# The experts' gathers without a bound: empty slots read the last row of the node table

## The chip, the cores and the metric

The kernel runs on one core of a Trainium2 chip. The metric is the device time of the whole program in microseconds. The core's engines are TensorE (PE; its weight loads are PEld), VectorE (DVE), ScalarE (ACT), GpSimd (POOL) and SyncE (SP); 16 DMA engines move data between HBM and the on-chip memories.

## The reference

A graph convolution over 6250 nodes with 256 features and 200000 edges, a mixture of 64 experts of which each node takes two, then two normalisations. Cut to what matters:

```python
h = feats * rsqrt(deg_out)[:, None]
m = segment_sum(h[src], dst) * rsqrt(deg_in)[:, None]
x = (m @ W_gc + b_gc) + (feats @ W_res + b_res)      # 6250 x 256: the node table
vals, idx = top_k(x @ Wg + bg, 2); gates = softmax(vals)
# every node's row goes to its two experts, at most 1024 rows each (CAP)
h1 = gelu(einsum('ecd,edh->ech', buf, w1) + b1)      # 64 experts, 256 -> 512
h2 = einsum('ech,ehd->ecd', h1, w2) + b2             # 512 -> 256
y = x + sum_k gate_k * h2[row of the node's k-th choice]
out = layernorm(feats + batchnorm(y) * gamma + beta)
```

A row of an expert's buffer that no node takes has no effect on the output.

## The kernel before

The program has four stages, one after the other.

**Degrees and table.** Histograms of `src` on TensorE give the out-degrees; the scaled node features go to HBM as `table`, of NPAD = 49 x 128 = 6272 rows of 256 floats (1 KB).

**Edges** (to about 2200 us). The 200000 edges lie in columns of 128. There are 1568 columns, 196 groups of CPG = 8; 200000 / 128 = 1562.5 columns hold edges, and the rest was filled with PAD_SRC = NPAD - 1 = 6271 (`dve.memset(raw_src[:, EB - 1, :], PAD_SRC)`, L706). GpSimd issues one indirect DMA per column (`gather`, L465), which fetches 128 rows of `table`, with no bound. TensorE adds them up by destination with one-hot matmuls (L1154). Whenever a tile of 128 nodes is complete, "ticks" on all engines compute its `x`, its experts and the ranks of its rows within them, and ScalarE stores `x` to HBM as `nodes` (L608), all 128 rows of each of the 49 tiles, so that row 6271 of `nodes` is written too.

**Slot tables.** One-hot matmuls (L1173) build in two PSUM banks, for each of 64 x 8 chunks of 128 slots, which node and which choice stand in each slot. VectorE makes two index tables of it (L963 to L976): `sidx`, the row of the result table `y2` that the slot's output goes to, and `gidx`, the row of `nodes` that it reads. An empty slot gets UNUSED = 1e6 in `sidx`, and a number far above the last row in `gidx`. `slots_ready` then lets GpSimd go on, and `tables_done` the others.

**Experts** (about 2229 to 2810 us). The choices are 2 x 6250 = 12500 in 64 experts, 195 on average. Each expert has MAIN = 3 chunks whose DMAs are always issued, and a loop for the chunks above the third (`extra_chunks`). For each expert:

- SyncE loads w1, w2 and b2 of the expert after next, double buffered by parity (`weights`, L375, L380, L381).
- GpSimd, in its own order: the extra chunks of expert e, the three gathers of expert e + 2 (`load_slots`, L489; behind `tokens_t`, which says that the buffer `xg` of that parity has been transposed), and the three scatters of expert e (`store_slots`, L499; each behind its `out_ready`). Both kinds carry a bound, with `oob_is_err=False`: an index above the bound moves nothing. The bound of the gathers is N - 1 = 6249, that of the scatters the last row of `y2`.
- TensorE (`expert`, from L1272): layer 1 of the chunks that hold rows (L1263), then the transposes of expert e + 1 (`transpose_tokens`, L1256; chunk by chunk behind `gathered[par][k]`, and of all three chunks, empty or not), then layer 2 (L1269).
- ScalarE applies gelu (L663), VectorE copies the transposed tokens to SBUF (L1003, L1004) and adds b2 (L1030).

Since a skipped slot leaves the buffer as it was, GpSimd clears `xg` and `xgx` once before the first gather, with two memsets (L477, L478). Both lie in `ring_low`, the buffers of the edge phase.

**Combination and normalisation** (from about 2820 us): the rows of `y2` are read back, weighted and added, and the two normalisations follow.

What sets the order around the change is each engine's own instruction stream; semaphores tie the streams together, and nothing is reordered.

Of the kernel before, what the change touches and what calls it, by code (L numbers as in the profile page):

```python
# [9 lines left out]
ALU = mybir.AluOpType  # L10
# [5 lines left out]
N, D, EDGES = 6250, 256, 200000  # L16
H, EX, TOPK, CAP = 512, 64, 2, 1024
# [3 lines left out]
NPAD = NT * P  # L21
# [18 lines left out]
PAD_SRC = NPAD - 1  # L40
# [17 lines left out]
def graph_moe_kernel(nc, x, src, dst, W_gc, b_gc, W_res, b_res, Wg, bg, w1, b1, w2, b2, gamma, beta, out):  # L58
    ctx = ExitStack()
    with ctx:  # L60
        def sb(name, shape, dt=F32):
            return ctx.enter_context(nc.sbuf_tensor(name, shape, dt))

        def sem(name):
            return ctx.enter_context(nc.semaphore(name))
# [85 lines left out]
        tok_f = hot_low[:, :, :].rearrange("p j d -> p (j d)")[:, 0:SC]  # L151
        tok_t = hot_low[:, :, :].rearrange("p j d -> p (j d)")[:, SC:2 * SC]
        gidx, sidx = slots[:, 0, :], slots[:, 1, :]
# [15 lines left out]
        def piece(n):  # L169
            taken_to[0] += n  # L170
            return arena[:, taken_to[0] - n:taken_to[0]]

        xg = piece(2 * MAIN * D).rearrange("p (b k d) -> p b k d", b=2, k=MAIN)
# [3 lines left out]
        xgx = piece(D)  # L177
# [8 lines left out]
        xtra_idx = sb("xtra_idx", [P, 2], I32)  # L186
# [43 lines left out]
        nd_pick, nd_rank, nd_sel, nd_slot = sem("nd_pick"), sem("nd_rank"), sem("nd_sel"), sem("nd_slot")  # L230
        y2_zeroed = sem("y2_zeroed")
        nd_stored = sem("nd_stored")
        slots_mm, tokens_clear, slots_ready = sem("slots_mm"), sem("tokens_clear"), sem("slots_ready")
        tables_done, gb_in, gap_ready, exp_ready = sem("tables_done"), sem("gb_in"), sem("gap_ready"), sem("exp_ready")
        b1_t = sem("b1_t")
        w1_in, w2_in, b2_in = ([sem(f"{w}_in{par}") for par in range(2)] for w in ("w1", "w2", "b2"))
        gathered = [[sem(f"gathered{par}{k}") for k in range(MAIN)] for par in range(2)]
# [6 lines left out]
        xtra_copied, xtra_gathered, xtra_t, xtra_s = sem("xtra_copied"), sem("xtra_gathered"), sem("xtra_t"), sem("xtra_s")  # L244
# [173 lines left out]
        def _(pool):  # L418
# [19 lines left out]
            pool.memset(acc_flat[:, 0:2 * COLS], 0.0).then_inc(acc_zero, 1)  # L438


            node_reg, row_reg = pool.alloc_register("last_node"), pool.alloc_register("last_row")
            pool.reg_mov(node_reg, N - 1)
            pool.reg_mov(row_reg, TOPK * NPAD - 1)
            last_node, last_row = node_reg, row_reg

            def start():
                pool.sem_inc(pool_starts, 1)
# [26 lines left out]
            pool.wait_ge(y2_zeroed, 16 * (TOPK * NPAD // P // 2))  # L474
            pool.wait_ge(nd_stored, 16 * NT + 16)
            pool.wait_ge(slots_mm, 1)
            pool.memset(xg[:, :, :, :], 0.0).then_inc(tokens_clear, 1)  # L477
            pool.memset(xgx[:, :], 0.0).then_inc(tokens_clear, 1)  # L478
            pool.wait_ge(tokens_clear, 2)
            pool.wait_ge(slots_ready, 1)  # L480

            def load_slots(e, par, first):

                if not first:
                    pool.wait_ge(tokens_t, e - 1)
                    start()
                for k in range(MAIN):
                    col = e * SLOTCH + k
                    pool.indirect_dma_start(  # L489
                        out=xg[:, par, k, :], out_offset=None, in_=nodes[:, :],  # L490
                        in_offset=bass.IndirectOffsetOnAxis(ap=gidx[:, col:col + 1], axis=0),
                        bounds_check=last_node, oob_is_err=False).then_inc(gathered[par][k], 16)

            def store_slots(e, par):
                for k in range(MAIN):
# [11 lines left out]
            def extra_chunks(e, nch):  # L507
                with pool.If(nch > MAIN):
                    with pool.Fori(MAIN, nch) as k:
                        col = nc.s_assert_within(k + e * SLOTCH, 0, SC - 1,  # L510
                                                 skip_runtime_bounds_check_because="no expert has more than SLOTCH chunks")
                        pool.reg_add(nextra, nextra, 1)
                        n = pool.snap(nextra, min_val=1, max_val=EX * SLOTCH)
                        pool.tensor_copy(xtra_idx[:, 0:1], gidx[:, bass.ds(col, 1)])
                        pool.tensor_copy(xtra_idx[:, 1:2], sidx[:, bass.ds(col, 1)]).then_inc(xtra_copied, 1)
                        pool.wait_ge(xtra_copied, n)
                        start()
                        pool.indirect_dma_start(
                            out=xgx[:, :], out_offset=None, in_=nodes[:, :],
                            in_offset=bass.IndirectOffsetOnAxis(ap=xtra_idx[:, 0:1], axis=0),  # L520
                            bounds_check=last_node, oob_is_err=False).then_inc(xtra_gathered, 16)
                        pool.wait_ge(xtra_out, n)
                        start()
                        pool.indirect_dma_start(
                            out=y2[:, :], out_offset=bass.IndirectOffsetOnAxis(ap=xtra_idx[:, 1:2], axis=0),
                            in_=outx[:, :], in_offset=None,
                            bounds_check=last_row, oob_is_err=False).then_inc(xtra_scattered, 16)
                        pool.wait_ge(xtra_scattered, n * 16)
                        start()

            def chunks_of(e):
                return pool.value_load(nch_i[0:1, e:e + 1], min_val=1, max_val=SLOTCH)

            load_slots(0, 0, True)
            load_slots(1, 1, True)
            pool.wait_ge(tables_done, 1)
            for e in range(EX):
                extra_chunks(e, chunks_of(e))
                if e + 2 < EX:
                    load_slots(e + 2, e % 2, False)  # L540
                store_slots(e, e % 2)
# [163 lines left out]
        def _(dve):  # L705
# [97 lines left out]
            a, k = 0, 1  # L803
            while k < GROUPS:
                dve.drain()
                dve.tensor_tensor(sfx[:, 1 - a, 0:GROUPS], sfx[:, a, 0:GROUPS], sfx[:, a, k:GROUPS + k], ALU.min)
                a, k = 1 - a, 2 * k
# [165 lines left out]
            dve.drain()  # L973
            dve.tensor_tensor(tok_f, tok_f, tok_t, ALU.add)
            dve.drain()
            dve.tensor_copy(gidx[:, :], tok_f).then_inc(slots_ready, 1)  # L976

            dve.tensor_scalar(nch_f[:, :], banks[5][0:1, 2 * P:2 * P + EX], float(CAP), float(P - 1), ALU.min, ALU.add)
            dve.drain()
# [391 lines left out]
```

## Time and profile before

| | us |
|---|---|
| median of 3 runs | 3005.2 |
| lowest and highest | 3001.09, 3006.76 |
| the profiled execution | 3007.82 |
| its span, first to last instruction | 3006.0 |

| engine | busy us | share of the span |
|---|---|---|
| TensorE matmuls | 2070.9 | 69% |
| GpSimd | 1948.3 | 65% |
| VectorE | 1251.7 | 42% |
| ScalarE | 395.3 | 13% |

The shares are means over stages with different limits: the edge phase is a steady stream of gathers on GpSimd, the experts' stage is denser on TensorE. A view by window tells one stage from another; the waits say who waited for whom; the chain of waits is the one path of work and waits that led to the end, so a delay counts there and not elsewhere.

### The profile page before, as it was taken

To read this page: it belongs to the slowest core of one execution; us is meant where nothing else is said; L and a number is where in the kernel's file an instruction comes from. 1 tells how busy PE (TensorE), PEld (TensorE's weight loads), DVE (VectorE), ACT (ScalarE), POOL (GpSimd) and SP (SyncE) were. 2 spreads that over 40 slices of the span, in tenths; PEclk is the share of its full clock that TensorE was granted. 3 is DMA by queue.
4 is the path that set the end of the run, shared out by engine and by line. 5 is a ranking of instruction groups with operands and counts; after the bars stand their busy time and mean duration, and the time that the engine had idled before them with its cause. 6 is when DMAs were issued, how large, how long until landed. Compare 5 with 4: busy or idle time off the path is not lost.

```text
span 3006.0 us, 44273 instructions
## 1 busy us (share of the span) xinstructions
PE 2070.9 (69%) x10262; PEld 1708.5 (57%) x10263; DVE 1251.7 (42%) x3095; ACT 395.3 (13%) x1350; POOL 1948.3 (65%) x1989
## 2 busy tenths in 40 slices
PE   7955656566666666666766777777768898989360
PEld 6954444444544455555555555655647787989250
DVE  9971112223233333444445444555542222222467
ACT  1010000000000000010111111111112222323013
POOL 2007777777777777777777777777725577777603
PEclk6557777777778788888889998999978899999685
DMA  8023333333333333333333333333424465656332
GB/s 291 0 95 106 107 106 106 106 107 107 107 108 109 108 109 108 109 109 111 109 109 111 111 111 111 111 111 111 111 72 138 147 192 179 199 182 196 107 121 85
DMA packets 205321, 363.40 MB, mean 121 GB/s; under 512 B 43160, under 2 KB 125894, under 8 KB 205054
## 3 DMA queue, kind: packets, MB, share of 16 engines
q0 software_dynamic: 93888, 231.34, 26.8%
q1 hardware_dynamic: 104058, 123.31, 12.8%
q10 hardware_dynamic: 7108, 6.43, 0.6%
q14 instruction: 250, 2.05, 0.2%
q8 instruction: 17, 0.28, 0.0%
HBM read 328.57 MB, written 57.52 MB: 128 GB/s over the span
## 4 chain that ended last, share of the span: by engine, by line
POOL 35%; PE 27%; issue 18%; DVE 8%; DMA 5%; DVEq 3%; ACT 1%; POOLq 1%; PEld 1%; ACTq 1%; SPq 0%; PEldq 0%
POOL ring L465 17%; POOL stage L465 17%; PE bank L1269 7%; PE bank L1154 6%; PE bank L1263 6%; PE bank L1134 3%; DMA ring<-nodes,slots 2%; PE bank L1194 2%; DVE acc L1047 1%; PE bank L1256 1%; DMA stage<-y 1%; PE bank L1173 1%; DVE stage L756 1%; DMA ring<-table,ring_idx 1%; DVE slots L856 1%
## 5 line engine op out<-in xcount | busy, mean ns | idle before, releaser
L465 POOL DMA_INDIRECT ring<-table,ring_idx x792 | 749.0, 946 | 241.8 <-issue 240.6
L465 POOL DMA_INDIRECT stage<-table,ring_idx x776 | 733.9, 946 | 236.3 <-issue 233.4
L1154 PE MATMUL bank<-ring,hot 128*128 128x257 f32 x1056 | 305.8, 452 | 166.8 <-DMA ring<-table,ring_idx 157.9
L1154 PE MATMUL bank<-stage 128*128 128x257 f32 x1040 | 305.9, 458 | 137.6 <-DMA stage<-table,ring_idx 128.9
L1154 PEld LDWEIGHTS bank<-ring,hot 128*128 128x128 f32 x1056 | 237.7, 231 | 229.0 <-issue 151.1
L1154 PEld LDWEIGHTS bank<-stage 128*128 128x128 f32 x1040 | 237.8, 234 | 200.0 <-issue 106.2
L952 DVE TENSOR_TENSOR acc<-acc,bank 128x257 f32 x196 | 82.9, 423 | 564.4 <-PE bank L1154 526.9
L499 POOL DMA_INDIRECT y<-ring,slots x192 | 193.3, 1007 | 98.3 <-issue 58.8
L1263 PEld LDWEIGHTS bank<-ring,stage 128*128 128x128 f32 x1984 | 236.9, 196 | 16.4 <-issue 11.8
L1263 PE MATMUL bank<-ring,stage 128*128 128x128 f32 x1984 | 241.0, 281 | 6.4 <-issue 3.7
L489 POOL DMA_INDIRECT ring<-nodes,slots x192 | 195.6, 1019 | 68.5 <-issue 55.6
L1269 PE MATMUL bank<-stage,ring 128*128 128x256 f32 x976 | 229.5, 389 | 7.5 <-ACT ring L663 7.5
L1154 PE MATMUL bank<-ring,stage 128*128 128x257 f32 x528 | 160.2, 469 | 105.1 <-DMA ring<-table,ring_idx 67.8
L1154 PE MATMUL bank<-stage,hot 128*128 128x257 f32 x512 | 157.5, 474 | 90.1 <-DMA stage<-table,ring_idx 84.4
L1269 PEld LDWEIGHTS bank<-stage,ring 128*128 128x128 f32 x976 | 185.7, 196 | 34.1 <-issue 10.2
L1154 PEld LDWEIGHTS bank<-ring,stage 128*128 128x128 f32 x528 | 124.0, 241 | 138.8 <-issue 58.4
L1154 PEld LDWEIGHTS bank<-stage,hot 128*128 128x128 f32 x512 | 121.7, 244 | 123.5 <-issue 79.3
L663 ACT ACTIVATE ring<-bank,b1e 128x128 f32<-128x128 f32 x488 | 139.1, 368 | 379.8 <-PE bank L1263 379.8
L589 ACT ACTIVATE ring_idx<-srcT 128x8 int32 (+1 forms) x198 | 40.1, 205 | 962.9 <-DMA ring<-table,ring_idx 487.9
L1134 PE MATMUL bank<-stage 128*128 128x49 bf16 x1568 | 159.9, 278 | 7.3 <-DVE stage L756 6.8
L1134 PEld LDWEIGHTS bank<-stage 128*128 128x128 bf16 x1568 | 153.0, 150 | 14.2 <-DVE stage L756 13.3
L1003 DVE COPY ring<-bank 128x512 f32<-128x512 f32 x64 | 44.2, 691 | 260.1 <-PE bank L1256 251.0
(230 smaller groups left out, 2551.0 us busy)
## 6 DMA issues: line engine op xcount, KB each, us to landing
stage<-in_L_gnn_w_dram SPq DMA_DIRECT2D x128, 512.0 KB
ring<-table,ring_idx POOLq DMA_INDIRECT x792
y<-zeros SPq DMA_DIRECT2D x49, 256.0 KB, 2.1
stage<-y SPq DMA_DIRECT2D x14, 896.0 KB, 7.3
stage<-table,ring_idx POOLq DMA_INDIRECT x776
stage<-in_L_gnn_b_dram SPq DMA_DIRECT2D x64, 128.0 KB
nodes<-yS ACTq DMA_DIRECT2D x49, 128.0 KB
xs<-in_x_dram SPq DMA_DIRECT2D x1, 6144.0 KB
```

Of the source, the lines that this page charges most:

```text
L465: pool.indirect_dma_start(out=ring(q)[:, j, 0:D], out_offset=None, in_=table[:, :], in_offset=bass.IndirectOffsetOnAxis(ap=ring_idx[:, q, ...
L489: pool.indirect_dma_start(out=xg[:, par, k, :], out_offset=None, in_=nodes[:, :], in_offset=bass.IndirectOffsetOnAxis(ap=gidx[:, col:col + ...
L499: pool.indirect_dma_start(out=y2[:, :], out_offset=bass.IndirectOffsetOnAxis(ap=sidx[:, col:col + 1], axis=0), in_=outs[:, par, k, :], in_ ...
L589: act.activation(ring_idx[:, q, :], srcT[:, bass.ds((it * RING + q) * CPG, CPG)], ACT.Copy).then_inc(idx_ready, 1)
L663: last = act.activation(h1[:, k, j, :], banks[2 + k][:, j * P:(j + 1) * P], ACT.Gelu, bias=b1e[:, j:j + 1])
L952: dve.tensor_tensor(acc[:, bass.ds(first_tile, 1), :], acc[:, bass.ds(first_tile, 1), :], banks[q % 2][:, 0:D + 1], ALU.add).then_inc(acc_ ...
L1003: dve.tensor_copy(xgT[:, 0:2, :, :], banks[0][:, :])
L1134: last = pe.matmul(banks[0][:, 0:HI], lo_hot[:, q, :, c], hi_hot[:, q, :, c], start=first and q == 0 and c == 0, stop=final and q == n - 1 ...
L1154: last = pe.matmul(bank[:, 0:D + 1], hots[:, j, :], ring(q)[:, j, :], start=j == 0, stop=j == CPG - 1)
L1194: last = pe.matmul(banks[4][:, a * D:(a + 1) * D], tS[:, a * DK + k, :], (wgc, wres)[a][:, k, :], start=k == 0, stop=k == DK - 1)
L1263: last = pe.matmul(bank[:, j * P:(j + 1) * P], w1s[:, par, c, j * P:(j + 1) * P], xt[:, c, :], start=c == 0, stop=c == DK - 1)
L1269: last = pe.matmul(dst, h[:, j, :], w2s[:, par, j, :], start=j == 0, stop=j == HK - 1)
```

## The change

Three things change, all at the start of the experts' stage and in its gathers.

1. The gathers of the experts' tokens (three per expert, and that of the extra chunks) lose `bounds_check` and `oob_is_err`, and so the register that held the bound goes.
2. The last operation of the chain that makes `gidx` is no longer a plain copy to int32 but a minimum with PAD_SRC = 6271, written as int32. An empty slot's index is thus 6271, the last row of `nodes`, and its gather reads that row.
3. The memsets of `xg` and `xgx` and the semaphore `tokens_clear` go, since every slot is now written by every gather.

The scatters keep their bound: an empty slot's output is still not stored.

```diff
-            node_reg, row_reg = pool.alloc_register("last_node"), pool.alloc_register("last_row")
-            pool.reg_mov(node_reg, N - 1)
-            pool.reg_mov(row_reg, TOPK * NPAD - 1)
-            last_node, last_row = node_reg, row_reg
+            last_row = pool.alloc_register("last_row")
+            pool.reg_mov(last_row, TOPK * NPAD - 1)
...
             pool.wait_ge(slots_mm, 1)
-            pool.memset(xg[:, :, :, :], 0.0).then_inc(tokens_clear, 1)
-            pool.memset(xgx[:, :], 0.0).then_inc(tokens_clear, 1)
-            pool.wait_ge(tokens_clear, 2)
             pool.wait_ge(slots_ready, 1)
...
                     pool.indirect_dma_start(
                         out=xg[:, par, k, :], out_offset=None, in_=nodes[:, :],
-                        in_offset=bass.IndirectOffsetOnAxis(ap=gidx[:, col:col + 1], axis=0),
-                        bounds_check=last_node, oob_is_err=False).then_inc(gathered[par][k], 16)
+                        in_offset=bass.IndirectOffsetOnAxis(ap=gidx[:, col:col + 1], axis=0)).then_inc(gathered[par][k], 16)
...
-                            in_offset=bass.IndirectOffsetOnAxis(ap=xtra_idx[:, 0:1], axis=0),
-                            bounds_check=last_node, oob_is_err=False).then_inc(xtra_gathered, 16)
+                            in_offset=bass.IndirectOffsetOnAxis(ap=xtra_idx[:, 0:1], axis=0)).then_inc(xtra_gathered, 16)
...
             dve.tensor_tensor(tok_f, tok_f, tok_t, ALU.add)
             dve.drain()
-            dve.tensor_copy(gidx[:, :], tok_f).then_inc(slots_ready, 1)
+            dve.tensor_scalar(gidx[:, :], tok_f, float(PAD_SRC), None, ALU.min).then_inc(slots_ready, 1)
```

GpSimd, between the last gather of the edges and the experts' first loads; `ring` is the memory of `xg` and `xgx`, `slots` that of `gidx`. Before:

```order
L465 DMA stage<-table,ring_idx 128x256 x7
L477 MEMSET ring 128x1536 [waits slots_mm,nd_stored,y2_zeroed]
L478 MEMSET ring 128x256
L489 DMA ring<-nodes,slots 128x256 [waits slots_ready,tokens_clear]
L489 DMA ring<-nodes,slots 128x256 x5
L532 TENSOR_LOAD nch_i [waits tables_done]
```

After:

```order
L463 DMA stage<-table,ring_idx 128x256 x7
L484 DMA ring<-nodes,slots 128x256 [waits slots_mm,slots_ready,nd_stored,y2_zeroed]
L484 DMA ring<-nodes,slots 128x256 x5
L525 TENSOR_LOAD nch_i [waits tables_done]
L525 ISA x2
```

The two memsets are gone, and the waits that stood before the first of them now stand before the first gather, beside `slots_ready`. The six gathers of experts 0 and 1 follow as before.

VectorE, the end of the chain that makes the index tables; `hot` is the memory of `tok_f` and `tok_t`. Before:

```order
L969 TENSOR_TENSOR hot<-hot 128x512
L971 CAST slots<-hot 128x512
L972 TENSOR_SCALAR hot<-hot 128x512
L974 TENSOR_TENSOR hot<-hot 128x512
L976 CAST slots<-hot 128x512
L978 TENSOR_SCALAR nch_f<-bank 1x64
```

After:

```order
L962 TENSOR_TENSOR hot<-hot 128x512
L964 CAST slots<-hot 128x512
L965 TENSOR_SCALAR hot<-hot 128x512
L967 TENSOR_TENSOR hot<-hot 128x512
L969 TENSOR_SCALAR slots<-hot 128x512
L971 TENSOR_SCALAR nch_f<-bank 1x64
```

One CAST has become one TENSOR_SCALAR at the same place; nothing else moves there, nor in the loop over the experts.

## Rows read from the trace of the kernel before

**Rows 1.** the page: busy time of the engines, and a group by line.
```profile
PE 2070.9 (69%) x10262; PEld 1708.5 (57%) x10263; DVE 1251.7 (42%) x3095; ACT 395.3 (13%) x1350; POOL 1948.3 (65%) x1989
...
L465 POOL DMA_INDIRECT ring<-table,ring_idx x792 | 749.0, 946 | 241.8 <-issue 240.6
```

**Rows 2.** windows, stage of the experts: columns stand in its first row.
```profile
core 0: us, PE busy (x) PEld busy (x) DVE busy (x) ACT busy (x) POOL busy (x), PEclk, DMA share, GB/s
2229.00:2806.00 577.00, 510.17 (x3352) 463.87 (x3353) 142.47 (x328) 155.11 (x558) 389.94 (x389) 0.94 0.56 174
2236.00:2238.00 2.00, 0.41 (x2) 0.22 (x2) 1.02 (x2) 0.00 (x0) 1.49 (x2) 0.50 0.02 0
2506.00:2513.00 7.00, 5.05 (x16) 4.33 (x17) 1.88 (x5) 0.00 (x0) 3.06 (x3) 0.52 0.12 32
...
2793.00:2797.00 4.00, 3.95 (x13) 3.33 (x14) 1.07 (x3) 0.00 (x0) 3.09 (x4) 0.57 0.35 113
```

**Rows 3.** groups of GpSimd, 2229 to 2812 us: xcount | busy us, mean ns | idle.
```profile
L489 POOL DMA_INDIRECT ring<-nodes,slots x192 | 195.6, 1019 | 68.5 <-issue 55.6 <-DVE ring L1030 7.9 <-DVE slots L976 4.1
L499 POOL DMA_INDIRECT y<-ring,slots x192 | 193.3, 1007 | 98.3 <-issue 58.8 <-DVE ring L1030 38.2 <-PE bank L1256 1.2
```

**Rows 4.** waits, 2229 to 2806 us: waiter <- waited for: us, times, longest us.
```profile
PEld bank L1256 <- DMA ring<-nodes,slots: 45.3, 26, 12.0
```

**Rows 5.** chain that ended last, 2190 to 2830 us: start us, us, what.
```profile
by line: PE bank L1269 32.1%; PE bank L1263 27.1%; DMA ring<-nodes,slots 11.1%; issue 7.5%; PE bank L1256 4.9%; POOL y L499 1.9%; POOLq L542 1.5%; POOL ring L489 1.5%; DVE ring L1030 1.3%; ACT ring L663 1.2%; DMA stage<-y 1.2%; PE bank L115
...
2228.97 5.60 DMA ring<-nodes,slots
...
2500.91 6.99 DMA ring<-nodes,slots
...
2559.66 2.91 DMA ring<-nodes,slots
...
2796.23 3.20 DMA ring<-nodes,slots
```

**Rows 6.** timeline at the stage's entry: start us, us, engine, instruction [idle before].
```profile
2223.29 1.38 POOL L477 MEMSET ring<- 128x1536 f32 x1 [45.83 <-PE bank L1246]
...
2226.38 0.42 DVE L972 TENSOR_SCALAR hot<-hot 128x512 f32<-128x512 f32 x1
2226.87 0.69 DVE L974 TENSOR_TENSOR hot<-hot 128x512 f32<-128x512 f32 x1
2227.64 0.43 DVE L976 CAST slots<-hot 128x512 int32<-128x512 f32 x1
...
2228.97 1.02 POOL L489 DMA_INDIRECT ring<-nodes,slots  x1 [4.05 <-DVE slots L976]
...
2235.50 1.00 POOL L489 DMA_INDIRECT ring<-nodes,slots  x1 [0.30 <-issue]
```

**Rows 7.** the page, DMA queues: packets, MB, share of 16 engines.
```profile
q0 software_dynamic: 93888, 231.34, 26.8%
```

**Rows 8.** windows, edge phase: a steady stretch, and its last gathers.
```profile
2180.00:2181.00 1.00, 0.41 (x3) 0.16 (x2) 0.79 (x1) 0.00 (x0) 0.00 (x0) 1.00 0.65 66
2000.00:2025.00 25.00, 19.57 (x92) 15.61 (x92) 14.97 (x46) 4.24 (x17) 18.91 (x20) 1.00 0.39 111
2174.00:2181.00 7.00, 5.62 (x26) 4.28 (x25) 5.57 (x11) 0.99 (x4) 2.84 (x3) 1.00 0.72 82
```

**Rows 9.** timeline, the last gather of the edges.
```profile
2176.51 0.95 POOL L465 DMA_INDIRECT stage<-table,ring_idx  x1 [0.30 <-issue]
```

**Rows 10.** timeline, a stall of TensorE for a gather, and what follows.
```profile
2500.91 1.00 POOL L489 DMA_INDIRECT ring<-nodes,slots  x1 [0.31 <-issue]
...
2507.95 0.29 PEld L1256 LDWEIGHTS bank<-ident,ring 128*128 128x128 f32 x2 [2.98 <-DMA ring<-nodes,slots]
...
2508.43 3.62 PE L1269 MATMUL bank<-stage,ring 128*128 128x256 f32 x8
...
2523.42 1.96 PE L1269 MATMUL bank<-stage,ring 128*128 128x256 f32 x8 [0.67 <-ACT ring L663]
```

More of the change, by code:

```diff
@@ L232, in graph_moe_kernel @@
         nd_stored = sem("nd_stored")
-        slots_mm, tokens_clear, slots_ready = sem("slots_mm"), sem("tokens_clear"), sem("slots_ready")
+        slots_mm, slots_ready = sem("slots_mm"), sem("slots_ready")
         tables_done, gb_in, gap_ready, exp_ready = sem("tables_done"), sem("gb_in"), sem("gap_ready"), sem("exp_ready")
```

## The prediction

> **What bounds the kernel now.** I read the page first: of the span of 3006.0 us TensorE is busy 2070.9 and GpSimd 1948.3 us [rows 1]. The change touches only the stage of the experts, so the windows view comes next: from 2229 to 2806 us TensorE is busy 510.17 us of 577, the 16 DMA engines 0.56 of the time at 174 GB/s, and the granted clock is 0.94 [rows 2]. GpSimd spends 195.6 us there on 192 gathers and 193.3 us on 192 scatters [rows 3]; with the 0.30 us between two issues an expert costs it 3 x (1.02 + 0.30) + 3 x (1.01 + 0.30) = 7.9 us, against 577 / 64 = 9.0 us per expert on the clock. So TensorE sets the pace where an expert has two or three chunks, and where several small experts follow one another GpSimd does. The waits view shows how the two meet: TensorE's weight loads wait 45.3 us in 26 waits for gathered tokens, 12.0 us of it once, at the start [rows 4]. The chain of waits is what I trust most: in order of time it goes 15 times through a piece "DMA ring<-nodes,slots" of 2.9 to 7.0 us, from the issue of a gather to its landing, 14 of them behind the first at 2228.97 [rows 5]. What lengthens those landings lengthens the kernel; what is saved on GpSimd elsewhere counts little, since its instructions and the issue gaps make only 1.9 + 1.5 + 7.5 = 10.9% of this stretch of the chain [rows 5].
>
> **The memsets.** Two fills leave GpSimd, one of 1.38 us [rows 6] and one of a sixth of its size. They end about 2225; then GpSimd stands 4.05 us idle until VectorE has written the indices (L976) and only then issues the first gather at 2228.97 [rows 6]. Their cover is VectorE's chain L963 to L976. Gain: 0. Without that cover it would be 1.7 us, once. The register moves and one semaphore wait that go with them are before the same idle time: 0.
>
> **The min in place of the cast.** L976 takes 0.43 us as a cast; L972, a TENSOR_SCALAR over the same 128x512, takes 0.42 us [rows 6]. No extra instruction is issued. Cost: 0, at most the 0.69 us of the two-operand L974, minus 0.43: 0.3 us once.
>
> **The bound.** No row of before shows an expert's gather without a bound. The nearest is the edges' gather, which has none: 946 ns [rows 1], against 1019 ns [rows 3]. That is 73 ns x 192 = 14.0 us of GpSimd's time; the other end is that the difference belongs to something else, 0. I take 73 ns, since the bounded scatters cost 1007 ns [rows 3] too. Little of it is on the path: for a gather on the chain it is 3 x 0.073 = 0.2 us for each of the three issues that stand before the last landing.
>
> **The empty slots.** 64 experts x 3 chunks x 128 slots are 24576, and 6250 nodes x 2 are 12500 choices, so about half, some 12,100, are empty (a few rows lie in fourth chunks). Today they move nothing: q0 carried 231.34 MB [rows 7]; the edges' 1568 gathers of 128 KB account for 205.5, the rest is 25.8, which is 12500 rows in and 12500 out at 1 KB (25.6). The sixth gather, the third chunk of expert 1, issued at 2235.50 [rows 6], is followed by 2 us with a DMA share of 0.02 and 0 GB/s [rows 2]. After the change each empty slot reads 1 KB, 12.4 MB more, and all of it from one row of the table, 6271. With 195 choices per expert, the third chunk is nearly always wholly empty and the second about half.
>
> **What reading one row costs.** The trace has this case already. Edges fill 1562.5 columns of 1568, and the rest hold PAD_SRC, so the last five gathers of the edge phase, one each 1.25 us and the last issued at 2176.51 [rows 9], read row 6271 of their table with all 128 indices. In a normal stretch a gather is issued every 1.25 us, 111 GB/s flow and the engines are busy 0.39 of the time [rows 8], that is 0.39 x 1.25 = 0.5 us per gather. From 2174 to 2181 us they are busy 0.72 and only 82 GB/s flow; in the microsecond from 2180, over 3 us after the last issue, 66 GB/s still do [rows 8]. 131072 bytes / 82 GB/s = 1.6 us for a gather of one row: three times a normal one.
>
> So the third chunk's gather, which is nothing today, gets 1.6 us; half of that falls to the second chunk's, which partly hides in the 1.3 us between issues. The bounds for one landing are 0.5 us (normal rate) and 1.6 + 0.8 = 2.4 us (nothing hides). I take 1.6. Less the 0.2 us of the bound, a gather on the chain lands 1.4 us later, and 14 x 1.4 = 19.6 us. The first piece, at 2228.97, runs beside the first weight loads; I count it in the range only.
>
> A rule that speaks for this stands in the Trainium skill, "DMA: Bandwidth & Descriptors", section "Latency and other measured facts": streams whose partitions lie at 4 MiB pitch in HBM run at half rate, 103 against 207 GB/s, put down there, as an inference, to lock-stepped streams meeting on one channel. The trace agrees in kind, for one row instead of a pitch: 82 against 111 GB/s at nearly twice the busy share. By that page's factor of two a one-row gather would cost 1.0 us and the sum would be 14 x 0.8 = 11 us.
>
> **The clock.** Each lengthened stall also lets TensorE's granted clock fall. Up to 2507.95 it waited 2.98 us; the clock over 2506 to 2513 is 0.52, and 8 matmuls of L1269 take 3.62 us where the eight at 2523.42 take 1.96 [rows 10]. The stretch from 2793 shows 0.57 [rows 2], behind a stall for a gather too. One fall costs some 1.5 us. Of the twelve other gathers on the chain I expect five to reach such lengths: 5 x 1.5 = 7.5 us; the bounds are 0 and 12 x 1.5 = 18.
>
> **Sum.** 19.6 + 7.5 = 27 us on the profiled 3007.8 us (its span 3006.0 and 1.8 around it). That execution lies 2.6 us over the median 3005.2; I add to the median: 3032 us.
>
> **Rivals.** (a) *Only the bytes count.* In the experts' stage the reads are mixed with weight loads, so 16 engines seldom meet on the row, and a wholly empty gather costs the normal 0.5 us. For it: half of the engines' time is free [rows 2]. Against it: the stalls lie just where everything is in flight at once. 14 x (0.5 - 0.2) = 4 us: 3009 us, no measurable change. The Trainium skill's formula on the same page ("Anatomy of one DMA": 2.0 us plus bytes / 436e3) would give 0.3 us for 128 KB and so 14 x 0.1 = 1.4 us; it belongs to this rival.
> (b) *GpSimd's saving wins.* The one-row reads stay within the time in which the landing waits for other traffic (the landing at 2507.95 of a gather issued at 2500.91 took 7.0 us [rows 10] with next to no bytes of its own), and only the 73 ns count: GpSimd's 10.9% of the 640 us that the chain's view covers are 70 us, of some 384 x 1.31 = 503 us that it spends on issuing, so 14.0 x 70 / 503 = 2 us, and 15 x 0.2 = 3 us on the gather pieces: 3000 us. It decides from the point at which an empty gather adds less than 0.2 us to a landing.
> (c) *Knock-on.* The slow reads hold the queues for the weights and the next chunk too, second chunk and third add in full, and experts that have slack today stall. Engines' time: 12.4 MB / 82 GB/s = 151 us on top of 0.56 x 577 = 323, or 82% of the stage. 20 pieces x 2.2 us + 10 falls x 1.5 us = 59 us: 3064 us.
>
> **How the numbers follow.** Forecast 0.58 (its own range 3013 to 3050), (a) 0.13, (b) 0.11, (c) 0.18. Times within about 0.2%, 6 us, can't be told from no change. (b) is faster by that in 0.07 and else the same; (a) is the same in 0.10; the forecast lies under 3011 in 0.02. That gives faster 0.07, same 0.16, slower 0.77. The range reaches from (a)'s lower side, 3004, into (c), 3056; about 0.1 stays out on each side.
>
> **What would show it.** Of after: gathers of 946 ns at the experts (the bound); q0 at 243.7 MB; a DMA share of 0.7 or more in the stage; TensorE's wait for gathers up from 45 us to 65 or more and the stage 20 to 30 us longer; more stretches with a granted clock near 0.57; every other stage unchanged. I am wrong if the wait for gathers stays under 50 us, or if an empty gather after the first lands as early as today.

## The result, and the profile after

The changed kernel takes 3017.2 us in the median of 8 runs (3014.07 to 3030.66), the kernel before 3002.7 us in the median of 8 (3000.41 to 3006.76). The ratio is 1.0054, with a 95% interval of 1.0038 to 1.0069: slower by 16 us, between 11 and 21. It was repeated twice later: 1.0039 [1.0026, 1.0052] and, in a pair that differs by the change alone, 1.0042 against 1.0004. So 11 to 16 us is what has to be explained.

The profiled execution of after took 3015.34 us, 1.9 under its median, that of before 3007.82 us, 5.1 over its median of 8. The two traces are therefore only 7.5 us apart, and sizes are better taken from the timed runs than from this one pair.

The page of after: busy time of the engines, the clock, DMA and GB/s over 40 slices of 75 us (slices 31 to 37 lie wholly in the stage of the experts), and the queue of the gathers.

```profile
PE 2075.6 (69%) x10214; PEld 1717.2 (57%) x10263; DVE 1251.8 (42%) x3095; ACT 395.5 (13%) x1350; POOL 1935.8 (64%) x1987
...
PEclk6557778787888888888889989999979999999685
DMA  8023333333333333333333333333435577766332
GB/s 290 0 96 106 107 106 105 106 108 108 107 108 110 108 109 109 108 111 109 109 111 110 111 110 111 112 111 112 104 98 160 164 212 209 214 198 209 114 117 85
...
q0 software_dynamic: 93888, 243.92, 28.7%
```

Against [rows 1] GpSimd is busy 12.5 us less; the edge phase is as it was. q0 carries 12.58 MB more than in [rows 7] in the same number of packets: the empty slots now move data.

The gathers of after (L484 was L489), then before's own entry in the same view: minimum, median and maximum duration in ns, first and last start, who waited for them, and how long they took to land. (The last line has this for 32 of the 192 only, the third chunks of every other expert.)

```profile
L484 POOL DMA_INDIRECT ring<-nodes,slots x192: 940/960/1010, 2229.4 to 2800.2; - x192
...
  PEld bank L1249: 54.8, 30
...
DMA to landing us min/median/max: 2.7/4.6/6.6
```

```profile
L489 POOL DMA_INDIRECT ring<-nodes,slots x192: 994/1017/1057, 2229.0 to 2796.2; - x192
```

The scatters of after, in the same view, and then those of before; the last scatter ends the stage.

```profile
L493 POOL DMA_INDIRECT y<-ring,slots x192: 982/1003/1022, 2248.6 to 2818.2; - x192
```

```profile
L499 POOL DMA_INDIRECT y<-ring,slots x192: 982/1002/1041, 2248.1 to 2811.8; - x192
```

A gather issues faster (median 960 ns against 1017), and yet TensorE's wait for gathers rises from 45.3 us [rows 4] to 54.8. From the first gather to the last scatter before needs 2811.8 - 2229.0 = 582.8 us and after 2818.2 - 2229.4 = 588.8.

Windows of the steady part of that stage, before and then after; columns as in [rows 2].

```profile
2240.00:2800.00 560.00, 500.39 (x3297) 455.23 (x3295) 137.75 (x315) 152.04 (x551) 377.89 (x377) 0.95 0.56 174
```

```profile
2240.00:2800.00 560.00, 493.27 (x3270) 449.73 (x3270) 136.19 (x310) 150.87 (x546) 364.85 (x374) 0.96 0.66 195
```

The chain that ended last, 2190 to 2850 us, of before and then of after: shares by line.

```profile
by line: PE bank L1269 31.1%; PE bank L1263 26.3%; DMA ring<-nodes,slots 10.8%; issue 7.3%; PE bank L1256 4.7%; DVE acc L1047 2.5%; POOL y L499 1.8%; POOLq L542 1.5%; POOL ring L489 1.4%; DVE ring L1030 1.2%; ACT ring L663 1.2%; DMA stage<-
```

```profile
by line: PE bank L1262 27.8%; PE bank L1256 24.8%; DMA ring<-nodes,slots 13.0%; issue 8.2%; PE bank L1249 4.7%; POOL ring L484 3.0%; POOL y L493 3.0%; DVE acc L1040 1.8%; POOLq L535 1.5%; DMA stage<-y 1.1%; DVE ring L1023 1.1%; PE bank L114
...
2314.87 5.94 DMA ring<-nodes,slots
...
2499.94 6.24 DMA ring<-nodes,slots
...
2635.13 6.63 DMA ring<-nodes,slots
...
2792.49 6.22 DMA ring<-nodes,slots
```

The path has moved from TensorE's matmuls (57.4% before, 52.6% after) to the landing of gathers (10.8% to 13.0%) and to GpSimd's own instructions and issue gaps (1.8 + 1.4 + 7.3 = 10.5% to 14.2%). The pieces "DMA ring<-nodes,slots" sum up to 71.1 us in 15 pieces before and 85.9 us in 16 after. So there is more waiting for landings, and GpSimd's own sequence, too, has a larger part of what ends last.

### The profile page after: what moved, and what is told of

Same layout as the page of the kernel before. It is cut to its first block, busy times and chain, and to the rows that moved or that the text cites. A ratio compares the mean times of both kernels' runs of the same rounds, so it can differ in the third digit from the quotient of the medians.

```text
span 3013.5 us, 44222 instructions
## 1 busy us (share of the span) xinstructions
PE 2075.6 (69%) x10214; PEld 1717.2 (57%) x10263; DVE 1251.8 (42%) x3095; ACT 395.5 (13%) x1350; POOL 1935.8 (64%) x1987
## 3 DMA queue, kind: packets, MB, share of 16 engines
q0 software_dynamic: 93888, 243.92, 28.7%
## 4 chain that ended last, share of the span: by engine, by line
POOL 36%; PE 26%; issue 19%; DVE 8%; DMA 5%; DVEq 3%; POOLq 1%; ACT 1%; PEld 1%; ACTq 0%; SPq 0%; PEldq 0%
POOL ring L463 18%; POOL stage L463 17%; PE bank L1262 6%; PE bank L1147 6%; PE bank L1256 5%; PE bank L1127 3%; DMA ring<-nodes,slots 3%; PE bank L1187 2%; DVE acc L1040 1%; PE bank L1249 1%; DMA stage<-y 1%; PE bank L1166 1%; DVE stage L749 1%; POOL ring L484 1%; POOL y L493 1%
## 5 line engine op out<-in xcount | busy, mean ns | idle before, releaser
L484 POOL DMA_INDIRECT ring<-nodes,slots x192 | 185.3, 965 | 118.1 <-issue 58.5
L1147 PE MATMUL bank<-ring,stage 128*128 128x257 f32 x528 | 167.9, 487 | 97.9 <-DMA ring<-table,ring_idx 59.5
```

Of the source, the lines that this page charges most:

```text
L484: pool.indirect_dma_start(out=xg[:, par, k, :], out_offset=None, in_=nodes[:, :], in_offset=bass.IndirectOffsetOnAxis(ap=gidx[:, col:col + ...
L1147: last = pe.matmul(bank[:, 0:D + 1], hots[:, j, :], ring(q)[:, j, :], start=j == 0, stop=j == CPG - 1)
```

## The experiments

The theory: the empty slots' reads of one common row delay the landing of a gather (some 22 us in all), and the missing bound gives a few us back. The rivals: the bytes alone do it, whichever row they come from; or the bound or the memsets matter more than thought.

### The change without its parts: row_bound, spread, spread_bound, and the change again

These four ran beside the same runs of before. `row_bound` reads the common row but keeps the bound, so that the reads stand alone:

```diff
-            pool.reg_mov(node_reg, N - 1)
+            pool.reg_mov(node_reg, NPAD - 1)
...
-            pool.memset(xg[:, :, :, :], 0.0).then_inc(tokens_clear, 1)
-            pool.memset(xgx[:, :], 0.0).then_inc(tokens_clear, 1)
-            pool.wait_ge(tokens_clear, 2)
...
-            dve.tensor_copy(gidx[:, :], tok_f).then_inc(slots_ready, 1)
+            dve.tensor_scalar(gidx[:, :], tok_f, float(PAD_SRC), None, ALU.min).then_inc(slots_ready, 1)
```

`spread` is the changed kernel with the same bytes from different rows: an empty slot in column c and partition p reads row 12 c + p, so that an empty gather reads 128 neighbouring rows.

```diff
-            dve.tensor_scalar(gidx[:, :], tok_f, float(PAD_SRC), None, ALU.min).then_inc(slots_ready, 1)
+            dve.tensor_scalar(spread, iota_s[:, :], 12.0, pcol[:, 0:1], ALU.mult, ALU.add)
+            dve.tensor_scalar(tok_t, tok_f, float(NPAD), 1.0e5, ALU.is_lt, ALU.mult)
+            dve.drain()
+            dve.tensor_tensor(tok_t, tok_t, spread, ALU.add)
+            dve.drain()
+            dve.tensor_tensor(gidx[:, :], tok_f, tok_t, ALU.min).then_inc(slots_ready, 1)
```

`spread_bound` has the same indices with the bound kept, as in `row_bound`. `after_again` is the changed kernel itself.

> The changed kernel again, on the same chip as the three variants beside it. Theory (one-row reads): the empty slots' reads of row 6271 take the DMA engines three times as long as normal ones, the third chunk lands later, TensorE waits longer; the lost bound gives back some 3 us. 12 to 18 us over before, ratio 1.004 to 1.006. Rival (bytes): the 12.4 MB as such cost it; the same ratio here, so this run only gives the level for the others.

> Empty slots read row 6271 as in the changed kernel, no memsets, but the gathers carry a bound again (6271, which nothing exceeds). Theory: gathers back at 1019 ns instead of 946 to 960, DMA share and rate as after; 2 to 4 us slower than the changed kernel, 16 to 20 us over before. Rival (the missing bound itself changes how the transfers run): close to before, within 5 us.

> As the changed kernel, without bound, but an empty slot of column c and partition p reads row 12 c + p, so that a gather reads up to 128 different rows: same bytes, no common row. Three more VectorE operations stand before slots_ready, 1.7 us on the path. Theory (one-row reads): an empty gather costs some 0.5 us of the engines instead of 1.6; 3004 to 3009 us against 3003 before, of which 1.7 is the added chain, and a DMA share in the stage of about 0.60 against 0.63. Rival (bytes): as the changed kernel plus 1.7 us, 3017 to 3020 us, DMA share 0.63.

> As spread, with the bound of 6271 on the gathers. Theory: gathers at 1019 ns instead of 946, 2 to 4 us slower than spread. Rival (GpSimd's 73 ns are never on the path): equal to spread within 1 us.

Measured, beside 3005.28 us of before (24 runs):

| | empty slots read | bound | median us | ratio to before |
|---|---|---|---|---|
| after_again | one row | no | 3015.1 | 1.0039 [1.0026, 1.0052] |
| row_bound | one row | yes | 3027.7 | 1.0070 [1.0054, 1.0085] |
| spread | many rows | no | 3008.8 | 1.0009 [0.9997, 1.0021] |
| spread_bound | many rows | yes | 3016.3 | 1.0036 [1.0022, 1.0050] |

Three forecasts were missed: `row_bound` came to 22 us over before and 13 over `after_again` in the medians (16 to 20 and 2 to 4 were expected), `spread_bound` to 7.5 us over `spread` (2 to 4), and `after_again` to 10 us over before (12 to 18).

The gathers and the chain's shares (2190 to 2850 us) of `row_bound`, then of `spread`, the latter with its window (columns as in [rows 2]) and its q0:

```profile
L486 POOL DMA_INDIRECT ring<-nodes,slots x192: 994/1017/1057, 2233.9 to 2817.6; - x192
...
  PEld bank L1253: 61.6, 32
...
by line: PE bank L1266 27.9%; PE bank L1260 22.9%; DMA ring<-nodes,slots 14.8%; issue 9.4%; PE bank L1253 4.4%; POOL ring L486 3.7%; POOL y L496 2.9%; POOLq L539 1.5%; DVE ring L1027 1.4%; DMA stage<-y 1.1%; PE bank L1151 1.1%; DMA ring<-no
```

```profile
L485 POOL DMA_INDIRECT ring<-nodes,slots x192: 942/961/1011, 2234.4 to 2795.8; - x192
...
  PEld bank L1255: 45.7, 25
...
by line: PE bank L1268 30.6%; PE bank L1262 26.9%; DMA ring<-nodes,slots 10.2%; issue 7.2%; PE bank L1255 4.7%; DVE acc L1046 2.5%; POOL y L494 2.0%; POOL ring L485 1.8%; POOLq L536 1.5%; DMA stage<-y 1.1%; PE bank L1153 1.1%; ACT ring L657
...
2240.00:2800.00 560.00, 499.02 (x3296) 455.34 (x3297) 138.83 (x316) 151.24 (x546) 369.80 (x380) 0.95 0.62 197
...
q0 software_dynamic: 93888, 243.92, 28.1%
```

Three readings follow. **The common row costs.** In the ratios one row against many is 0.0030 without the bound (9 us) and 0.0034 with it (10 us; the medians differ by 6 and 11), and `spread` even carries three more VectorE operations ahead of its first gather, 1.9 us that only it and `spread_bound` pay. The bytes are equal. The wait for gathers falls back to 45.7 us, the figure of [rows 4], and the share of landings on the chain to 10.2%, that of before. **The bound costs more than forecast.** Bound against none is 0.0031 with one row (9 us) and 0.0027 with many (8 us; 13 and 7.5 in the medians); each difference is uncertain by about 6 us, both together by about 4. **Reads alone**, with the bound as before, cost 21 us [16, 26] (`row_bound`).

Worked out from the issue and the landing of every gather in the traces, the median time of a third chunk's gather is 2.7 us in before, 4.2 in after and in row_bound, and 3.0 in spread and spread_bound; that of a first chunk's is 3.6 to 3.8 us in all five. A second chunk's goes from 3.1 us to 3.7 in after and in row_bound, and to 3.4 and 3.1 in the two spread kernels. So the third chunk, mostly empty, lands 1.4 to 1.5 us later with the common row, of which 0.3 come with different rows too; the second chunk, empty in 17 experts, lands 0.6 us later.

**What the reads cost the DMA engines** follows from q0. From [rows 7] to the page of after its share goes from 26.8% to 28.7% of the span, some 59 us of all 16 engines for 12.58 MB more, or 0.6 us for 128 KB. In `spread` the same bytes take about 40 us, 0.4 us for 128 KB.

### The memsets alone: no_clear

Before without the memsets and their semaphore. Slots that are empty then hold what the buffer held; no stored row depends on them.

```diff
-            pool.memset(xg[:, :, :, :], 0.0).then_inc(tokens_clear, 1)
-            pool.memset(xgx[:, :], 0.0).then_inc(tokens_clear, 1)
-            pool.wait_ge(tokens_clear, 2)
```

> The kernel before without its two memsets and their wait; skipped slots leave what the edge phase left in the buffer, which reaches no output. Theory: the memsets end 4 us before the indices are ready, so nothing changes, within 3 us of before. Rival (they are on the path): 1.7 us faster, which this run can't tell from none; over 5 us faster would speak against the theory.

Measured: 3005.7 us, ratio 1.0000 [0.9985, 1.0014]. The memsets cost nothing that shows, within some 4 us, as forecast. The timeline of after says the same in its own way: VectorE's minimum takes 0.43 us, like the cast in [rows 6], and the first gather starts at 2229.36, not earlier than before's.

```profile
2228.02 0.43 DVE L969 TENSOR_SCALAR slots<-hot 128x512 int32<-128x512 f32 x1
...
2229.36 0.94 POOL L484 DMA_INDIRECT ring<-nodes,slots  x1 [51.63 <-DVE slots L969]
2230.60 0.95 POOL L484 DMA_INDIRECT ring<-nodes,slots  x1 [0.30 <-issue]
```

The 51.63 us in brackets are GpSimd's whole idle time there; in before the memsets had cut it into 45.83 and 4.05.

### The third chunk alone: third_row

`row_bound`, but only the third chunks' empty slots read row 6271; those of the first two are still skipped.

```diff
-            dve.tensor_copy(gidx[:, :], tok_f).then_inc(slots_ready, 1)
+            dve.tensor_copy(gidx[:, :], tok_f)
+            dve.drain()
+            third = lambda t: t.rearrange("p (e k) -> p e k", k=SLOTCH)[:, :, 2]
+            dve.tensor_scalar(third(gidx), third(tok_f), float(PAD_SRC), None, ALU.min).then_inc(slots_ready, 1)
```

> As row_bound (which was 21 us over before), with the bound of 6271, but only the empty slots of each expert's third chunk read row 6271; those of the first two chunks keep their index above the bound and move nothing. One VectorE operation of 0.2 us more before slots_ready. Theory (the third chunk lands last, and its 1.6 us count): most of row_bound's loss stays, 13 to 19 us over before. Rival (the second chunk's reads push the third's back, and the sum counts): 5 to 12 us.

Measured: 3022.5 us against 3005.9 (17 runs), ratio 1.0050 [1.0033, 1.0066]: 15 us of `row_bound`'s 21, for 7.6 of the 12.6 MB. q0 in its page:

```profile
q0 software_dynamic: 93888, 238.94, 28.2%
```

The median of a third chunk's gather is 4.1 us here and that of a second chunk's 3.0, as before. So most of the price hangs on the third chunk, as forecast, though not out of all proportion to its bytes: it has 60% of them. The intervals of the two kernels overlap; the remaining 6 us for the second chunks are not proved. The mean granted clock of these six runs is 0.826, against 0.831 for the 17 of before beside them, and no run of the six is above 0.828. A part of the price is therefore lost clock.

### Not gathering the empty chunks: skip_before and skip_after

If the gathers and scatters of empty chunks cost time on the path, leaving them out should gain, and it should take away what the bound is worth. Second and third chunks are gathered, transposed, completed and scattered only where `nch` (the expert's number of chunks) says that they hold rows; the waits count what was issued. The core of the edit, on GpSimd and TensorE:

```diff
                 for k in range(MAIN):
+                    if first or k == 0:
+                        fetch(k)
+                    else:
+                        with pool.If(ahead > k):
+                            fetch(k)
...
+                    if k == 0 or e < 2:
+                        put()
+                    else:
+                        with pool.If(nch > k):
+                            put()
...
+                        with pe.If(ahead > k):
+                            last = turn()
```

> The kernel before, where chunks 2 and 3 of an expert are gathered, transposed and scattered only if they hold rows (the experts 0 and 1 aside); the counts to wait for run in registers. Some 67 of 189 gathers and as many scatters go (52 third chunks, 16 second ones). Theory (GpSimd's issue rate and the landing of the third chunk set the pace where experts are small): per expert with two chunks GpSimd needs 5.3 us instead of 7.9, the waits of TensorE for gathers go from 45 to under 20 us, 15 to 30 us faster than before. Rival (branches and register loads on GpSimd and TensorE cost as much): within 6 us of before.

> The changed kernel with the same branches: a chunk without rows is not gathered, so only the empty slots of partly filled chunks read row 6271 (about 3,900 instead of 12,100). Theory: the one-row reads that are left cost little, and with the bound gone it comes within 4 us of skip_before, on either side. Rival (one-row reads cost in whatever chunk they are): 6 us or more slower than skip_before.

Measured: `skip_before` 2992.3 us, ratio 0.9953 [0.9936, 0.9969]; `skip_after`, the same with the change, 2994.9 us, ratio 0.9957 [0.9941, 0.9973]. The former beats both kernels, before by 14 us and after by some 27. Its q0, its windows (columns as in [rows 2]) and the chain from 2190 to 2850 us:

```profile
q0 software_dynamic: 87456, 231.27, 26.9%
```

```profile
2240.00:2800.00 560.00, 497.26 (x3225) 447.46 (x3224) 118.96 (x255) 154.88 (x559) 252.44 (x252) 0.97 0.56 176
```

```profile
by line: PE bank L1326 33.1%; PE bank L1320 32.9%; issue 7.8%; DMA ring<-nodes,slots 3.8%; DVE acc L1083 3.5%; PE bank L1301 3.3%; DMA stage<-y 2.2%; POOLq L564 1.2%; PE bank L1190 1.1%; ACT ring L685 1.0%; POOL y L511 1.0%; DVEq L1086 0.7%
```

Only 125 gathers are left of 192. GpSimd is busy 252 us there instead of 378, and landings make 3.8% of the chain instead of 10.8%. TensorE's weight loads wait 24.7 us for gathers instead of 45.3:

```profile
PEld bank L1301 <- DMA ring<-nodes,slots: 24.7, 11, 12.2
```

Both the gain (15 to 30 us were expected) and the wait (under 20) just miss their forecasts. Once the empty chunks are gone, the change no longer shows: the two ratios are 0.0004 apart, with some 5 us of uncertainty. So the empty chunks cost time already before the change, when they moved nothing. Which of their parts did, these two kernels don't tell: with the gathers go their scatters and their transposes, and TensorE's busy time in the page falls from 2070.9 [rows 1] to 2057.6 us, about as much as was gained.

```profile
PE 2057.6 (69%) x10080; PEld 1697.4 (57%) x10129; DVE 1229.5 (41%) x3028; ACT 396.0 (13%) x1350; POOL 1814.0 (61%) x1855
```

### How much of GpSimd's pace counts: two doses that gave no answer

The bound's 8 to 9 us on the path are most of the 10.4 us of GpSimd's time that it costs. To see whether GpSimd's pace as such counts that much, one more small instruction was put ahead of each expert's gathers, in before and in after. First a memset of one column:

```diff
+                pool.memset(neg_base[:, e:e + 1], 0.0)
```

> The kernel before with one more small GpSimd instruction per expert, a memset of one column ahead of its three gathers, of some 0.1 to 0.3 us with its gap: about what the bound costs an expert, 3 x 0.054 = 0.16 us. Theory A (an expert's GpSimd time is on the path in nearly all the 33 to 40 experts that follow each other at GpSimd's pace): an added 0.2 us per expert makes the kernel 7 to 10 us slower. Theory B (the prediction's: only the time around the gathers of the chain and 14% of the rest count): 3 us or less.

> The changed kernel with the same memset per expert. Theory A: 0.2 us per expert cancel what the missing bound gave back, so it comes to 3022 to 3028 us, near row_bound (1.007), against 1.0039 to 1.0054 of the changed kernel. Theory B: within 3 us of the changed kernel, a ratio of 1.004 to 1.006.

Measured beside 3010.21 us: 3013.4 us (1.0004 [0.9991, 1.0016]) and 3022.1 us (1.0042 [1.0028, 1.0055]). The groups of GpSimd in the stage show the dose:

```profile
L487 POOL MEMSET neg_base<- 128x1 f32 x64 | 8.3, 129 | 6.8 <-DVE slots L977 3.3 <-DMA y<-mS,xtra_idx 3.3 <-issue 0.2
```

It takes 129 ns but lies within the 0.30 us between two issues, so an expert's turn on GpSimd grew by 0.02 us only (7.91 to 7.93 us, median of the spacings): too small a dose to say anything. It does repeat the comparison of the change, +0.38%. The second dose was larger, with a semaphore that makes its order fixed:

```diff
+                pool.wait_ge(padded, e)
+                pool.memset(dstT[:, 0:D], 0.0).then_inc(padded, 1)
```

> The memset of pace_before lay in the idle gap between two issues and lengthened an expert's GpSimd time by 0.02 us only. Here it is 128x256 (0.31 us in the trace of before), which should add 0.16 to 0.2 us per expert, 11 us of GpSimd's time over the stage, as much as the bound costs (10 us). Theory A (GpSimd's pace is on the path in the 40 experts that follow each other at 7.9 us): 6 to 10 us slower than before. Theory B (the prediction's share): 3 us or less.

> The same on the changed kernel: 0.16 to 0.2 us per expert cancel the 0.16 us that the missing bound gave back. Theory A: a ratio of 1.0065 to 1.008, as row_bound's 1.007. Theory B: within 3 us of the changed kernel, 1.004 to 1.0055.

These ran on another chip, where the kernel before itself takes 3775.9 us (23 runs): 3768.3 us, ratio 0.9982 [0.9961, 1.0003], and 3778.5 us, ratio 1.0009 [0.9992, 1.0026]. In the stage of the experts GpSimd is not the pace there: the gathers of one expert follow those of the last at 10.0 us in the median, and the scatters of `pace2_before` wait 150.3 us for VectorE's results, against 38.2 us in [rows 3]:

```profile
L502 POOL DMA_INDIRECT y<-ring,slots x192 | 193.7, 1009 | 199.3 <-DVE ring L1033 150.3 <-issue 48.7 <-PE bank L1259 0.3
```

So this answers nothing for the first chips. Between its two kernels there are 0.27%, the change's own direction, but the two intervals overlap; that it costs there too is not shown.

## Why the prediction was right in direction and twice too large

**The empty slots, right in sum and partly by luck.** The forecast took 1.6 us for one landing and 14 landings on the path, 22.4 us before the bound is credited. `row_bound`, which has just this, costs 21 us, and the third chunk's landing grew by 1.4 to 1.5 us. Three things behind that agreement are not as forecast.

First, the landings that were on the path did not each come 1.6 us later. The chain of `row_bound` has 18 pieces of 5.4 us in the mean against 15 of 4.7, so 0.7 us more for each and three more of them. The forecast had given all fourteen the price of an empty third chunk. Traced to their experts, only 11 of the 15 pieces of before are third chunks, and three of these hold rows (experts 20, 35 and 50, for which `skip_before` still issues the gather).

Second, 1.6 us is not what the read costs the DMA engines. The prediction set bytes over rate, 131072 / 82e3 = 1.6 us, against busy share times spacing, 0.39 x 1.25 = 0.5 us. In like terms the tail's price is 0.72 x 1.6 = 1.15 us, little more than twice a normal gather's, and in the experts' stage it is 0.6 us for 128 KB. The reads thus took 59 us of the engines and not rival (c)'s 151. Why an empty gather lands 1.4 us later for 0.6 us of engine time no run shows.

Third, part of the 21 us may be clock, see below.

That the row counts beside the bytes is shown by the spread pair: 9 and 10 us between one row and many, plus the 1.9 us that the spread kernels pay in front. The bytes alone (`spread_bound` against before, 11 us less those 1.9) are about 9 us, with 5 us of uncertainty, so which is the larger part is open; the forecast's two prices, 0.5 us of a normal gather and 1.1 us more for one row, give 7 and 15. The Trainium skill ("DMA: Bandwidth & Descriptors", "Latency and other measured facts") has half the rate for streams at a 4 MiB pitch, 103 against 207 GB/s. By that factor the estimate was 14 us before the bound is credited (11 with it), where `row_bound` measured 21. The page speaks of another pattern, and this trace agrees with the factor in kind only: in the experts' stage the common row takes 0.6 us of the engines for 128 KB against 0.4 from different rows, a factor of about 1.6.

**The path, right in kind.** The chain's pieces of landing time sum up, over 2190 to 2850 us: 71.1 us in before, 67.8 in no_clear, 67.5 in spread, 73.5 in spread_bound, 83.0 in third_row, 84.1 and 85.9 in the two profiles of after, 97.8 in row_bound. The kernels whose third chunks read the common row are those with 83 and more (one profile each, two of after). The first gather to the last scatter takes 582.8, 578.3, 579.4, 585.3, 595.4, 590.1 and 588.8, 602.0 us in the same order.

**The bound, mis-sized: this is one half of the error.** The gathers take 965 ns in the mean, not 946, so the bound is 54 ns each and 10.4 us in all (forecast 73 and 14.0).

```profile
L484 POOL DMA_INDIRECT ring<-nodes,slots x192 | 185.3, 965 | 118.1 <-issue 58.5 <-DVE slots L969 51.6 <-DVE ring L1023 5.5
```

But the kernel's time shows about 8 to 9 of these 10.4 us, against the forecast's 0.2 us for each landing, 3 in all. The step that failed is "Little of it is on the path": it counted the bound only where the chain of before shows a landing, at 0.2 us each. GpSimd's share of the chain does rise when landings are late (10.5% in before, 14.2% in after, 3.7 + 2.9 + 9.4 = 16.0% in row_bound), but that is not the reason: with many rows, where the share is 2.0 + 1.8 + 7.2 = 11.0% in `spread` and 8.7% in `spread_bound`, the bound costs 8 us as well. The spacings of the experts' gathers are the better hint. 41 of the 63 in before are under 8.2 us, with a median of 7.92, which is GpSimd's own pace; in after 33 are, at 7.74, and in row_bound as many, at 7.91. 33 x 0.17 = 5.6 us and 41 x 0.17 = 7 us are less than 8 to 9 but within the uncertainty of 4. The size is measured; that it works through the pace is argued from these spacings and was not shown, since both doses gave no answer. A rival stands beside it, the clock: between 2250 and 2810 us the profile of row_bound has 10 to 17 us more at the low clock than the two of after, and that of spread_bound 10 us more than that of spread. At the low clock, 1.2 instead of 2.4 GHz, half of that time is lost at most, 5 to 8 us, and single profiles can't tell whether the bound brings it about.

**The clock, wrong for the change itself: the other half.** I had added five more falls of the granted clock, 7.5 us. The mean of the stage is 0.96 in after and 0.95 in before, where five more falls would have lowered it. From the clock records between 2250 and 2810 us there are 7 falls in before and 8 in after. The wait of after that answers to [rows 10]:

```profile
2506.22 0.29 PEld L1249 LDWEIGHTS bank<-ident,ring 128*128 128x128 f32 x2 [3.64 <-DMA ring<-nodes,slots]
...
2506.71 3.52 PE L1262 MATMUL bank<-stage,ring 128*128 128x256 f32 x8
```

It waited 3.64 us instead of 2.98 and then paid the same 3.5 us for eight matmuls as before did with 3.62: here a wait behind which the clock was low already cost nothing more when it grew. With the bound kept it is different: the windows view of `row_bound` shows 0.94,

```profile
2240.00:2800.00 560.00, 490.82 (x3213) 446.54 (x3213) 132.72 (x302) 147.60 (x535) 366.19 (x366) 0.94 0.63 189
```

and its low-clock time from 2250 to 2810 us is 65 us against 51 in before and 48 and 55 in the two profiles of after. Its 14 us over before are worth at most 7 us. The timed runs say the same more weakly: 0.828 for the six of row_bound against 0.830 for before, with `third_row`'s 0.826 against 0.831 as the clear case. So part of the clock's term is probably inside row_bound's 21 us, and the 21 us are then less pure a measure of the reads than they look.

**The sum again.** 21 us for the reads with what clock they cost, less 9 for the bound, 0 for the memsets and the minimum: 12 us, against 11 to 16 measured. Since the 9 is the difference between `row_bound` and `after_again`, this sum comes out for `after_again` by itself; only the first pair's 16 us and the later pair's 11 test it. The forecast was 22.4 - 3 + 7.5 = 27.

**The marks that I named.** q0 at 243.7 MB (243.92) and an unchanged edge phase came as said. Gathers of 946 ns came as 965. The DMA share is 0.66 and not 0.7 or more, since 128 KB of the reads cost 0.6 us of the engines; TensorE's wait for gathers is 54.8 us and not 65; the stage is longer by 6 to 7 us in two profiles, which lie low, and not by 20 to 30.

**The rivals.** *Only the bytes count* falls, since `spread` has the same bytes and costs 9 us less than after; but the bytes' own price, some 9 us with the bound kept, is as large as the row's. *GpSimd's saving wins* is refuted in its result, but its saving is real, 8 to 9 us where it had 5. The *knock-on* did not come in its size: a first chunk's gather lands as early as before (3.7 us). A small part of it is there, since the second chunk lands 0.6 us later and three more landings are on the path in `row_bound`.

## What to carry to other kernels

Count an empty gather as work: here one common row for all padding cost more than as many different rows, and, with the bound kept, both cost more than an index that is skipped. The best was not to issue it, together with its scatter and transposes, where the number of full chunks is known. Do not price a saving by the chain's share alone: the bound's 54 ns counted almost in full, though the chain of before gave GpSimd 11%. Compare like with like, bytes over rate with bytes over rate and engine time with engine time. And look at each wait before adding a clock penalty: here one that already had the low clock behind it paid no more when it grew.

## What the runs showed of the hardware

- Sixteen DMA engines that read one row of 1 KB are slow at it: 82 GB/s at a busy share of 0.72 in the last edge gathers of before [rows 8], and again in after (0.76, 84 GB/s), against 111 GB/s at 0.39 normally. Mixed with weight loads in the experts' stage, such reads take 0.6 us of the engines for 128 KB, against 0.4 us for as many different rows (`spread`).

```profile
2174.00:2181.00 7.00, 5.65 (x25) 4.34 (x24) 4.73 (x7) 0.99 (x4) 2.83 (x3) 1.00 0.76 84
```

- A bound on a gather of 128 rows costs 54 ns of GpSimd's time in the same place (965 against 1019 ns). A gather with all indices beyond the bound still takes 2.6 us to land in before (median of 50 empty third chunks), though it moves next to nothing; reading the common row it takes 4.3 us in after.
- A GpSimd instruction of 0.13 us fits into the 0.30 us between two indirect DMAs nearly for nothing: 0.02 us more for an expert (`pace_before`).
- One and the same program takes 3005 us on one chip and 3776 on another. What makes the other slower no run shows; on it the experts follow one another at 10.0 us in the median (`pace2_before`) against 7.9 (before).
